# Layer 0's head loop in another order on all engines: row-tile products in fours next to a key tile's sums, the next batch's queries one head earlier

## What is computed

```python
xn = layernorm(x)
x = x + L0_attn(xn) + L0_ffn(xn)        # L0_attn: 16 heads of width 8 that share one key and one value head
...
# L0_ffn, with H = 8 heads, E = 8 experts, P = 128, top-2 gates:
q = einsum('bsd,hpd->bhsp', x, q_w);  k = einsum('bsd,hpd->bhsp', x, k_w)
xv = einsum('bsd,hedp->bshep', x, v_w)
v = einsum('bshep,bshe->bhsp', xv, gate_v)
att = softmax(einsum('bhqp,bhkp->bhqk', q, k) * SCALE)
ctx = einsum('bhqk,bhkp->bqhp', att, v)
weighted = ctx[:, :, :, None, :] * gate_o[..., None]
out = einsum('bshep,hepd->bsd', weighted, o_w)
```

## Time and profile before

| | |
|---|---|
| median of 3 runs | 3204.99 us (3203.18 to 3208.26) |
| span of the profiled execution, first to last instruction | 3174.5 us |
| median less span | 30.5 us |
| PE busy | 3005.8 us, 95% of the span |
| DVE busy | 2399.0 us, 76% |
| POOL busy | 1836.4 us, 58% |
| ACT busy | 1620.3 us, 51% |
| granted PE clock, mean | 0.975 |

### The profile page before, as it was taken

One profiled execution on the slowest core, in us unless ns is written; L12 is line 12 of the kernel. 1 busy time (PEld: TensorE's weight loads), 2 busy tenths in 40 slices (PEclk: granted clock), 3 DMA queues, 4 the chain that ended last, 5 costly groups with the idle time before them and its releaser, 6 DMA issues. The chain is left out here.

```text
span 3174.5 us, 51808 instructions
## 1 busy us (share of the span) xinstructions
PE 3005.8 (95%) x17486; PEld 2083.7 (66%) x17486; DVE 2399.0 (76%) x4551; ACT 1620.3 (51%) x3277; POOL 1836.4 (58%) x2277
## 2 busy tenths in 40 slices
PE   4999999999999999999999999999999977899997
PEld 2666666666666666666666666666666655566674
DVE  7888888888888888888888888888888745144343
ACT  1455555555555555555555555555555532444634
POOL 2556666666666666666666666666666634444330
PEclk7999999999999999999999999999999988899999
DMA  5000000110100011111100110011001011133322
GB/s 167 21 22 22 22 22 22 32 32 23 36 22 22 22 32 32 28 29 36 29 22 22 32 32 22 23 36 28 23 22 39 8 23 58 45 111 103 91 77 85
DMA packets 139849, 124.63 MB, mean 39 GB/s; under 512 B 28410, under 2 KB 122116, under 8 KB 139492
## 3 DMA queue, kind: packets, MB, share of 16 engines
q1 hardware_dynamic: 125892, 88.46, 10.2%
q0 software_dynamic: 10160, 30.17, 3.0%
q10 hardware_dynamic: 3536, 2.69, 0.5%
HBM read 97.49 MB, written 29.30 MB: 40 GB/s over the span
## 5 line engine op out<-in xcount | busy, mean ns | idle before, releaser
L1210 DVE TENSOR_REDUCE m_peaks<-m_ring 128x1 f32<-128x512 f32 x1024 | 641.0, 680 | 117.9 <-PE m_ring L293 112.6
L957 ACT ACTIVATE m_expA<-m_ring 128x512 f32<-128x512 f32 x1024 | 538.5, 602 | 370.0 <-PE m_sums L381 178.6
L849 POOL TENSOR_TENSOR m_vprod<-m_vprod 128x512 f32<-128x512 f32 x256 | 353.6, 1381 | 510.5 <-DVE m_vprod L1223 509.2
L858 POOL TENSOR_TENSOR m_oprod<-m_oprod 128x512 f32<-128x512 f32 x256 | 328.2, 1282 | 279.2 <-DVE m_oprod L1290 279.2
L928 ACT ACTIVATE m_prob<-m_ring,m_negs 128x512 f32<-128x512 f32 x512 | 347.1, 684 | 243.1 <-DVE m_negs L1257 242.9
L344 PE MATMUL m_ring<-m_probT,m_vs 128*128 128x256 f32 x2048 | 467.0, 381 | 0.0
L344 PEld LDWEIGHTS m_ring<-m_probT,m_vs 128*128 128x128 f32 x2048 | 384.3, 190 | 79.8 <-issue 27.7
L1251 DVE TENSOR_REDUCE m_negs<-m_ring 128x1 f32<-128x512 f32 x512 | 340.7, 685 | 92.9 <-PE m_ring L99 92.0
L1290 DVE TENSOR_TENSOR m_oprod<-m_ring,m_go 128x512 f32<-128x512 f32 x512 | 341.3, 686 | 56.3 <-PE m_ring L99 52.3
L1223 DVE TENSOR_TENSOR m_vprod<-m_ring,m_gate 128x512 f32<-128x512 f32 x512 | 336.6, 683 | 43.9 <-POOL m_vs L851 27.0
L938 ACT ACTIVATE m_probT<-m_ring 128x512 f32<-128x512 f32 x512 | 283.8, 598 | 57.2 <-PE m_ring L332 54.1
(11 more groups left out here) (312 smaller groups left out, 5629.4 us busy)
## 6 DMA issues: line engine op xcount, KB each, us to landing
m_wraw<-in_v_w SPq DMA_DIRECT2D x32, 512.0 KB, 4.1
m_qf<-q_dram SPq DMA_DIRECT2D x128, 128.0 KB, 2.6
m_wraw<-in_o_w SPq DMA_DIRECT2D x32, 512.0 KB, 4.2
q_dram<-m_kf SPq DMA_DIRECT2D x24, 256.0 KB, 3.0
listed<-in_pad SPq DMA_DIRECT2D x6, 897.0 KB, 11.7
m_xg<-listed SPq DMA_DIRECT2D x39, 138.0 KB, 2.3
m_rows<-answers SPq DMA_DIRECT2D x8, 512.0 KB, 4.2
sums_dram<-m_sumsT ACTq DMA_DIRECT2D x128, 18.0 KB
```

What stands on the lines that cost most here:

```text
L849: vchain(pool.tensor_tensor(vprod[:, 0:512], vprod[:, 0:512], vprod[:, 512:1024], ALU.add))
L858: ochain(pool.tensor_tensor(op[:, 0:512], op[:, 0:512], op[:, 512:1024], ALU.add))
L957: act.activation(expA[hh][:, c * 512:(c + 1) * 512], ring.home["scT", n, k, hh, c][:, :], ACT.Exp)\
L1210: v.tensor_reduce(peaks[:, t, hh, c:c + 1], ring.home["peaks", n, t, hh, c][:, :], AX.X, ALU.max)\
```

## The change

PE's list is written in a new order with the same calls; the row-tile products of a token tile or key tile now stand four in a row, and next to `sum_by_key` in most places. The loop's cut is at another place, so it runs from -2 to N0 + 2. DVE's, ACT's and POOL's lists are rearranged as well, with the same calls, but that DVE's minimum of two halves is a call of its own. The queries of the next batch go from heads 4 and 5 of a batch to heads 3 and 4, on PE, ACT and SP.

```diff
@@ PE, batch_work (ACT's has keep_queries in the same place)
-                    if s in (4, 5) and place == 0:
-                        queries(after, s - 4)
+                    if s in (3, 4) and place == 0:
+                        queries(after, s - 3)
@@ SP
-                    if s in (5, 6):
-                        store_queries(after, s - 5)
+                    if s in (4, 5):
+                        store_queries(after, s - 4)
@@ DVE, find_largest
-                    if c:
-                        v.wait_ge(half_found, 2 * k + 2)
-                        if k >= 2:
-                            v.wait_ge(probs_made, 2 * (k - 1))
-                        v.tensor_tensor(neg[t % 2], half_neg[:, t % 2, 0:1], half_neg[:, t % 2, 1:2], ALU.min)\
-                            .then_inc(largest_found, 1)
+
+                def join_largest(n, t):
+                    if n not in steps:
+                        return
+                    k = TPB * n + t
+                    v.wait_ge(half_found, 2 * k + 2)
+                    if k >= 2:
+                        v.wait_ge(probs_made, 2 * (k - 1))
+                    v.tensor_tensor(neg[t % 2], half_neg[:, t % 2, 0:1], half_neg[:, t % 2, 1:2], ALU.min)\
+                        .then_inc(largest_found, 1)
```

PE's whole new list:

```diff
-                for i in range(-1, N0 + 2):
+                for i in range(-2, N0 + 3):
+                    outputs(i - 2, 7, 1)
+                    sum_by_key(i - 1, 2)
+                    peak_scores(i, 3, 0, 0)
+                    peak_scores(i, 3, 0, 1)
+                    peak_scores(i, 3, 1, 0)
+                    peak_scores(i, 3, 1, 1)
+                    weigh(i - 1, 0)
+                    scores_by_key(i - 1, 3, 0, 0)
+                    scores_by_key(i - 1, 3, 0, 1)
+                    scores_by_key(i - 1, 3, 1, 0)
+                    scores_by_key(i - 1, 3, 1, 1)
+                    turn(i - 1, 3, 0)
+                    turn(i - 1, 3, 1)
+                    outputs(i - 1, 0, 0)
+                    outputs(i - 1, 0, 1)
+                    scores(i - 1, 4, 0)
+                    scores(i - 1, 4, 1)
+                    peak_scores(i, 4, 0, 0)
+                    peak_scores(i, 4, 0, 1)
+                    peak_scores(i, 4, 1, 0)
+                    peak_scores(i, 4, 1, 1)
+                    weigh(i - 1, 1)
+                    turn(i - 1, 4, 0)
+                    peak_scores(i, 5, 0, 0)
+                    peak_scores(i, 5, 0, 1)
+                    peak_scores(i, 5, 1, 0)
+                    peak_scores(i, 5, 1, 1)
+                    sum_by_key(i - 1, 3)
+                    scores_by_key(i - 1, 4, 0, 0)
+                    scores_by_key(i - 1, 4, 0, 1)
+                    scores_by_key(i - 1, 4, 1, 0)
+                    scores_by_key(i - 1, 4, 1, 1)
+                    values(i, 3, 1)
+                    scores(i - 1, 5, 0)
+                    scores(i - 1, 5, 1)
+                    outputs(i - 1, 1, 0)
+                    outputs(i - 1, 1, 1)
+                    turn(i - 1, 4, 1)
+                    values(i, 4, 0)
+                    turn(i - 1, 5, 0)
+                    peak_scores(i, 6, 0, 0)
+                    peak_scores(i, 6, 0, 1)
+                    peak_scores(i, 6, 1, 0)
+                    peak_scores(i, 6, 1, 1)
+                    sum_by_key(i - 1, 4)
+                    scores_by_key(i - 1, 5, 0, 0)
+                    scores_by_key(i - 1, 5, 0, 1)
+                    scores_by_key(i - 1, 5, 1, 0)
+                    scores_by_key(i - 1, 5, 1, 1)
+                    outputs(i - 1, 2, 0)
+                    batch_work(i - 2, 2)
+                    batch_work(i - 2, 3)
+                    turn(i - 1, 5, 1)
+                    values(i, 4, 1)
+                    make_y(i, 0)
+                    scores(i - 1, 6, 0)
+                    values(i, 5, 0)
+                    outputs(i - 1, 2, 1)
+                    scores(i - 1, 6, 1)
+                    values(i, 5, 1)
+                    outputs(i - 1, 3, 0)
+                    sum_by_key(i - 1, 5)
+                    scores_by_key(i - 1, 6, 0, 0)
+                    scores_by_key(i - 1, 6, 0, 1)
+                    scores_by_key(i - 1, 6, 1, 0)
+                    scores_by_key(i - 1, 6, 1, 1)
+                    weigh(i - 1, 2)
+                    peak_scores(i, 7, 0, 0)
+                    peak_scores(i, 7, 0, 1)
+                    peak_scores(i, 7, 1, 0)
+                    peak_scores(i, 7, 1, 1)
+                    turn(i - 1, 6, 0)
+                    scores(i - 1, 7, 0)
+                    make_y(i, 1)
+                    scores(i - 1, 7, 1)
+                    values(i, 6, 0)
+                    outputs(i - 1, 3, 1)
+                    values(i, 6, 1)
+                    outputs(i - 1, 4, 0)
+                    sum_by_key(i - 1, 6)
+                    scores_by_key(i - 1, 7, 0, 0)
+                    scores_by_key(i - 1, 7, 0, 1)
+                    scores_by_key(i - 1, 7, 1, 0)
+                    scores_by_key(i - 1, 7, 1, 1)
+                    turn(i - 1, 6, 1)
+                    batch_work(i - 2, 0)
+                    scores(i, 0, 0)
+                    values(i, 7, 0)
+                    scores(i, 0, 1)
+                    values(i, 7, 1)
+                    turn_peaks(i, 0)
+                    outputs(i - 1, 4, 1)
+                    turn(i - 1, 7, 0)
+                    scores(i, 1, 0)
+                    turn_peaks(i, 1)
+                    scores(i, 1, 1)
+                    turn(i - 1, 7, 1)
+                    scores(i, 2, 0)
+                    batch_work(i - 1, 1)
+                    turn(i, 0, 0)
+                    scores(i, 2, 1)
+                    turn(i, 0, 1)
+                    weigh(i - 1, 3)
+                    turn(i, 1, 0)
+                    peak_scores(i + 1, 0, 0, 0)
+                    peak_scores(i + 1, 0, 0, 1)
+                    peak_scores(i + 1, 0, 1, 0)
+                    peak_scores(i + 1, 0, 1, 1)
+                    sum_by_key(i - 1, 7)
+                    scores_by_key(i, 0, 0, 0)
+                    scores_by_key(i, 0, 0, 1)
+                    scores_by_key(i, 0, 1, 0)
+                    scores_by_key(i, 0, 1, 1)
+                    values(i + 1, 0, 0)
+                    values(i + 1, 0, 1)
+                    turn(i, 1, 1)
+                    outputs(i - 1, 5, 0)
+                    scores(i, 3, 0)
+                    scores(i, 3, 1)
+                    outputs(i - 1, 5, 1)
+                    values(i + 1, 1, 0)
+                    sum_by_key(i, 0)
+                    scores_by_key(i, 1, 0, 0)
+                    scores_by_key(i, 1, 0, 1)
+                    scores_by_key(i, 1, 1, 0)
+                    scores_by_key(i, 1, 1, 1)
+                    turn(i, 2, 0)
+                    values(i + 1, 1, 1)
+                    outputs(i - 1, 6, 0)
+                    outputs(i - 1, 6, 1)
+                    turn(i, 2, 1)
+                    peak_scores(i + 1, 1, 0, 0)
+                    peak_scores(i + 1, 1, 0, 1)
+                    peak_scores(i + 1, 1, 1, 0)
+                    peak_scores(i + 1, 1, 1, 1)
+                    sum_by_key(i, 1)
+                    scores_by_key(i, 2, 0, 0)
+                    scores_by_key(i, 2, 0, 1)
+                    scores_by_key(i, 2, 1, 0)
+                    scores_by_key(i, 2, 1, 1)
+                    values(i + 1, 2, 0)
+                    outputs(i - 1, 7, 0)
+                    values(i + 1, 2, 1)
+                    peak_scores(i + 1, 2, 0, 0)
+                    peak_scores(i + 1, 2, 0, 1)
+                    peak_scores(i + 1, 2, 1, 0)
+                    peak_scores(i + 1, 2, 1, 1)
+                    values(i + 1, 3, 0)
```

DVE's new list from the end of head i's outputs 7 to peak tile 6, with `lower_ctx` and the reductions of two of the bursts, and POOL's new list:

```diff
+                    gate_values(i + 2, 2, 1)
+                    take_peaks(i + 2, 2, 0, 0)
+                    take_peaks(i + 2, 2, 0, 1)
+                    take_peaks(i + 2, 2, 1, 0)
+                    take_peaks(i + 2, 2, 1, 1)
+                    take_peaks(i + 2, 3, 0, 0)
+                    take_peaks(i + 2, 3, 0, 1)
+                    gate_values(i + 2, 3, 0)
+                    gate_outputs(i, 7, 1)
+                    take_peaks(i + 2, 3, 1, 0)
+                    take_peaks(i + 2, 3, 1, 1)
+                    lower_ctx(i + 1, 0)
+                    gate_outputs(i + 1, 0, 0)
+                    output_gates(i + 1, 1)
+                    gate_outputs(i + 1, 0, 1)
+                    find_largest(i + 1, 4, 0)
+                    find_largest(i + 1, 4, 1)
+                    take_peaks(i + 2, 4, 0, 0)
+                    join_largest(i + 1, 4)
+                    take_peaks(i + 2, 4, 0, 1)
+                    take_peaks(i + 2, 4, 1, 0)
+                    batch_work(i, 3)
+                    take_peaks(i + 2, 4, 1, 1)
+                    lower_ctx(i + 1, 1)
+                    take_peaks(i + 2, 5, 0, 0)
+                    take_peaks(i + 2, 5, 0, 1)
+                    take_peaks(i + 2, 5, 1, 0)
```

(58 more changed lines are left out.)

387 lines of the change are left out of this document (126 added, 261 removed).

## The result

The changed kernel takes 3169.73 us (median of 4 runs, 3167.05 to 3180.40) against 3205.23 us before: a ratio of 0.9884, 95% interval 0.986 to 0.9908, or -35.5 us. Forecast were 3159 us, -46. On a second chip the ratio was 0.9890 (0.9872 to 0.9908), -38.5 us.

What follows compares the result with a forecast made beforehand. TensorE's order of work was taken to set the time, with VectorE having 10 to 12 us a step to spare. Neighbours -29 and waits -17 gave -46 us, span 3128, median 3159 us; range 3108 to 3208, chance 0.42.

Steps and rivals of the forecast that it cites:

- the fill: Start of layer 0's head loop, one mostly empty iteration more at each end: zero, within 3 us.
- The two long runs: TensorE's runs of six and seven products, 1.20 and 1.28 us against 0.67 by price: their 1.1 us a step of waits goes.
- Neighbours: TensorE's same 148 calls a step, repriced by what stands beside each: -0.9 us a step, -29 us for 32 heads.
- part 3: The other engines' reordered lists, with the minimum as its own call and GpSimd mixing values and outputs: costed at nothing.
- The waits: TensorE's waits in a head's step fall from 2.7 to 2.2 us: -0.5 a step, -17 us.
- The four bursts: At peak tiles 0, 1, 5, 6: four peaks, sums, four key products; charged 0.15 us each, 0.6 a step.
- the walk: Two stretches, around `weigh(0)` and from there to peak tile 6, followed by durations: nothing late by a tile, margins 0.1 to 0.2.
- Part 4: Next batch's queries moved from heads 4 and 5 to 3 and 4: nothing either way.
- The 30.5 above the span: Median 3205.0 us lies 30.5 above the profiled span 3174.5; kept for the forecast, span 3128 becoming median 3159.
- (a): Rival: most TensorE waits vanish, 2.7 to 1.2 us a step; -77 us, 3128 us; chance 0.16.
- (b): Rival: VectorE takes the gain back in the 12 heads with gates; -28 us, 3177 us; chance 0.18.
- (c): Rival: VectorE comes a tile late to each burst, stall 0.63 us; +17 us, 3222 us; chance 0.14.

Runs made afterwards that it cites:

- b_again: The kernel before, unedited, run and profiled a second time: 3212.4 us, ratio 1.0008 to the kernel before.
- a_join_in_find: The changed kernel with the minimum of the two halves put back inside the second search: 3187.7 us, ratio 0.9933 to the kernel before.
- a_again: The changed kernel, unedited, run and profiled a second time: 3176.0 us, ratio 0.9890 to the kernel before.
- b_split_runs: The kernel before with its runs of six and seven products split by the key tile sums beside them: 3189.4 us, ratio 0.9942 to the kernel before.

## Why the prediction was right, and where its terms were off

The case named likeliest is the one that happened: the loop lost 42 us against 46 forecast, the median 36 to 38. The way there was another than forecast: a step lost 1.67 us, not 1.44, and the fill, which was set at nothing, took some 5 us of it back.

- **What bounds it.** TensorE's order does: putting `sum_by_key` in another place among the same calls moved the 28 steps by -23 in one kernel and +97 in the other.
- **The two long runs.** Working: -1.1 of waits and two more runs at 0.21 each, so -0.68 a step. Measured alone: -0.81.
- **The drain goes by the run.** Runs of two, three and four all take 0.43. By the Trainium skill's tail of 31 ns for each product that increments a semaphore (TensorE: Matmul & The Clock Gate, "The cost: per-tile semaphore tail") a run of four would be 0.06 longer than one of two, an estimate; start to start the trace has 0.00 to 0.01. Leaving the rule out was right for these prices.
- **Neighbours, and some luck.** What the change brings beyond the split runs is 24.0 us in 28 steps; the prediction's terms give 28 x (-1.4 + 0.68) = -20. That these agree is partly luck: if the pieces add, 14.1 of the 24.0 come from the minimum as a call of its own, which the prediction set at nothing, and some 11 us are lost again to GpSimd's order, which it set at nothing too (both under part 3). No run changes the neighbours alone, so their sum stays argued from the prices. `weigh` ahead of a turn, the item without a row, takes 758.03 - 754.50 = 3.53 where 3.37 is the price behind a run, and 3.46 behind a turn where 3.27 is the price: 0.16 and 0.19, not 0.1 each, 4 us in all.
- **The waits.** Predicted 2.2 a step, of which 1.6 was left standing and 0.6 charged to the bursts. Means over 27 steps, above the price: key products of tile 0 0.64, of tile 6 0.52, second `weigh` 0.40, peaks 0 behind a turn 0.13, key products 5 0.10, 2 and 4 0.09: 1.9. The four bursts were charged 0.60 and cost 0.83. Nearly all of this falls on tile 0, where the walk did not look, and it is not new: the same four products took 1.05 in b_again, 0.61 above the price. The other three bursts add 0.2. Tile 6 and the `weigh`, 0.92 together, stood in no term (tile 6's key products took 0.44 in b_again). The total came near because about 1.0 of other old waits went as these came (2.7 less 1.1 and 0.61, an estimate), which the prediction did not work out.
- **Part 3, at nothing: wrong twice.** The minimum as a call of its own is worth 12 to 14 us, a third of the gain. The prediction saw what a later minimum could cost a softmax and not what it spares VectorE: 0.30 us each time it no longer stands directly behind the search. (4.1 of the 14 us fall in the one step in which the clock fell.) And with GpSimd's new order, mixing values and outputs, VectorE waits 1.43 us once a step, which reaches TensorE as 0.40, 11 us in 28 steps. This chain is read from the timelines; no run put GpSimd's order back. "Out of 10 idle" was a mean; just there nothing was idle. (That the 0.40 would go with outputs 6 summed in the 3 us in which GpSimd stands idle before, was not tried.)
- **Part 4, at nothing.** Right in both directions.
- **Fill.** Some 5 us longer, outside the 3 allowed, nearly all of it ahead of head 0's first `scores` product; its cause is open.
- **The 30.5 above the span, let stand.** Right for the median and wrong for the span: 3128 was forecast and 3165.2 measured, 4.5 below the median. The 30.5 was not around the span but inside it. The part behind the loop of the profiled execution before was 581 us, of b_again 618, and the changed kernel has the longer form too. In the list of who waited for whom, ScalarE's longest of these in b_again and then in the changed kernel; the first profile before has none over 10.9 at this place:

```profile
ACT m_hT L2453 <- remote: 47.1, 2, 36.8
```

```profile
ACT m_hT L2464 <- remote: 46.7, 2, 37.6
```

- **The rivals.** (a), 28 steps some 67 us shorter, fell by the 1.9 of waits. (b) is half true: by b_again's steps less the changed kernel's, heads 10 to 13 and 18 to 21 gained 0.9 a step, heads 3 to 5, which have gates too, 1.8, the others 2.0; VectorE, busy 72 of 78 us in head 12, probably takes back half of the gain there and not all of it; no run took the gates out. The 4 us of waits that (b) saw in head 12's step were not all waits: the step took 79.9 us at a mean clock of 0.98 in the earlier trace rows and 78.8 at 1.00 in b_again. (c) needed 0.5 at each burst; the mean is 0.2.
- **Signs.** "16 runs of 0.44, none of 1.2" held within 0.1 for 13 of 16 (not for the key products of tiles 0 and 6 and the peaks of tile 4). The eighth product came after 1.44 to 1.48 us on the mean in three bursts, after 1.75 in that of tile 0.

## What to carry to other kernels

Price an order of work from start to start, with its neighbours, and look for runs that are longer than the buffers in front of them: splitting two runs gave half of this gain. A tiny operation that stands directly behind the one it depends on costs its engine the wait for that result; let one independent operation stand between, even where the engine seems to have time. A wait that is taken out is worth what the place puts in its stead: four tries aimed at real waits of 0.3 to 0.6 us a step each gave nothing or cost time. An engine's idle average does not tell whether it is free in the moment before a burst.

## What was not expected of the hardware

- A stall of TensorE can be paid twice. In head 25's step it stood idle 2.44 us (busy 3.56 of 6 us, mean clock 0.73 in them, 1.00 before), and the granted clock was 0.55 on the mean from 2036 to 2040, so for most of it at the lower level of 1.2 GHz: the next two blocks took 1.45 and 1.28 instead of 0.78 and 0.69, in all some 2 us beyond the stall. In a_join_in_find the same followed in head 13's step (0.57 and then 0.50 from 1116 to 1123), after TensorE had stood idle 1.33 us ahead of the peaks of tile 0; in a_again it was idle 0.53 there and the clock stayed at 1.00.
- Behind the loop ScalarE stands up to 38 us for something that the profile puts down to no engine of the core ("remote"). Twelve of the fourteen executions profiled have it. In b_split_runs the profile puts a wait of 39.7 us at the same line down to a TensorE product instead, and only the first one before has none over 10.9; its part behind the loop was at least 26 us shorter. What ScalarE waits for is open, and so is whether this wait makes the difference.
